# Softmax sums of a self-attention group inverted in a 128x8 tile that DMAs fill and empty

## The reference, cut to what matters

```
scores = jnp.einsum('bhqd,bhkd->bhqk', q, k) / math.sqrt(HD)
attn = jax.nn.softmax(scores, axis=-1)
out = jnp.einsum('bhqk,bhkd->bhqd', attn, v)
```

## Time and profile before

| | us |
|---|---|
| median of 3 runs | 260.71 |
| lowest, highest | 259.54, 261.23 |
| the profiled execution | 261.54 |
| its span, first to last instruction | 259.4 |

### The profile page before, as it was taken

One profiled execution on the slowest core, in us unless ns is written; L12 is line 12 of the kernel. 1 busy time (PEld: TensorE's weight loads), 2 busy tenths in 40 slices (PEclk: granted clock), 3 DMA queues, 4 the chain that ended last, 5 costly groups with the idle time before them and its releaser, 6 DMA issues.

```text
span 259.4 us, 4344 instructions
## 1 busy us (share of the span) xinstructions
PE 239.6 (92%) x1563; PEld 171.6 (66%) x1563; DVE 196.5 (76%) x351; ACT 132.2 (51%) x285; POOL 103.3 (40%) x135
## 2 busy tenths in 40 slices
PE   7999999988997799998999999999999999989971
PEld 4478797754654457675666767677776777668850
DVE  1377577899765899869889998986669895897574
ACT  1545377566368366556467656654435533313430
POOL 7297400000114307745466555556255533001362
PEclk9999999999999899999999999999999999999995
DMA  6999940000000840000000000000000000000011
GB/s 246 321 278 322 412 167 0 4 1 3 0 3 0 158 86 0 3 0 0 5 0 0 3 0 0 0 3 0 0 3 0 1 3 1 0 3 0 1 40 40
DMA packets 4500, 13.65 MB, mean 53 GB/s; under 512 B 512, under 2 KB 1280, under 8 KB 4352
## 3 DMA queue, kind: packets, MB, share of 16 engines
q1 hardware_dynamic: 4048, 11.29, 13.1%
q0 software_dynamic: 432, 2.10, 3.7%
HBM read 14.43 MB, written 0.52 MB: 58 GB/s over the span
## 4 chain that ended last, share of the span: by engine, by line
PE 71%; DVE 13%; DMA 5%; ACT 4%; issue 2%; SPq 2%; POOL 1%; POOLq 0%; DVEq 0%; ACTq 0%
PE ps L844 11%; PE ps L794 7%; PE ps L821 5%; PE ps L858 5%; PE ps L822 5%; PE ps L795 5%; PE ps L778 5%; DMA wq<-in_wq 5%; PE ps L634 3%; PE ps L923 3%; DVE mneg L1350 3%; PE ps L831 2%; PE ps L696 2%; PE ps L681 2%; PE ps L574 2%
## 5 line engine op out<-in xcount | busy, mean ns | idle before, releaser
L1184 ACT ACTIVATE probs<-ps 128x512 f32<-128x512 f32 x64 | 38.0, 597 | 46.7 <-PE ps L822 45.8
L1412 DVE TENSOR_REDUCE xmneg<-ps 128x1 f32<-128x512 f32 x64 | 43.0, 688 | 16.2 <-PE ps L795 15.8
L445 POOL TENSOR_TENSOR psums<-psums,probs 128x512 f32<-128x512 f32 x30 | 38.6, 1288 | 10.8 <-ACT probs L1184 8.3
L441 POOL TENSOR_TENSOR psums<-probs 128x512 f32<-128x512 f32 x15 | 19.2, 1281 | 43.1 <-ACT probs L1184 43.1
L794 PE MATMUL ps<-KA,QA 128*128 128x512 f32 x64 | 30.3, 474 | 2.8 <-DVE xmneg L1412 1.9
L844 PE MATMUL ps<-probs,kv_dup 128*64 128x256 f32 x256 | 31.2, 385 | 0.0
L1430 DVE RECIPROCAL xrcp<-ps 128x256 f32<-128x256 f32 x16 | 28.0, 1751 | 1.9 <-PE ps L831 1.9
L1176 ACT ACTIVATE QA<-ps 64x256 fp32r<-64x256 f32 x64 | 24.2, 378 | 10.1 <-PE ps L778 8.9
L1350 DVE TENSOR_REDUCE mneg<-ps 128x4 f32<-128x1024 f32 x16 | 19.6, 1224 | 9.4 <-PE ps L574 9.0
L821 PE MATMUL ps<-QA,KA 128*128 128x512 f32 x64 | 26.0, 406 | 0.0
L398 POOL TENSOR_TENSOR rstd<-mv,eps_col 128x1 f32<-128x1 f32 x12 | 2.3, 189 | 59.4 <-DVE mv L1338 59.1
(11 more groups left out here) (162 smaller groups left out, 459.7 us busy)
## 6 DMA issues: line engine op xcount, KB each, us to landing
wu<-in_wu SPq DMA_DIRECT2D x4, 640.0 KB, 8.9
wq<-in_wq SPq DMA_DIRECT2D x4, 512.0 KB, 13.4
wcT<-in_wcT SPq DMA_DIRECT2D x4, 384.0 KB, 12.3
wE<-in_wE SPq DMA_DIRECT2D x4, 320.0 KB, 11.2
w13T<-in_w POOLq DMA_DIRECT2D x1, 1024.0 KB, 8.2
x1T<-in_xT SPq DMA_DIRECT2D x1, 512.0 KB, 3.7
kvp<-in_kv POOLq DMA_DIRECT2D x1, 512.0 KB, 6.1
x_nat<-in_xn SPq DMA_DIRECT2D x1, 512.0 KB, 18.6
```

What stands on the lines that cost most here:

```text
L445: g.tensor_tensor(psums[:, s, :], psums[:, s, :], probs[:, s, kc, :], ALU.add).then_inc(xadd_sb, 1)
L1184: a.activation(probs[:, n % 2, kc, :], ps[:, 2 + u % 2, :], ACT.Exp).then_inc(xexp_sb, 1)
L1412: v.tensor_reduce(xmneg[:, n % 4, qt, hh:hh + 1], ps[:, u % 2, :], AX.X, ALU.max, negate=True).then_inc(xmax_sb, 1)
```

## The change

For seven of the eight groups (`TURNED`) the order is turned round: the sums are inverted first and spread afterwards. SP sends the four sum rows of `CT` (one partition, 256 elements each) by four DMAs into `sum_cols`, a tile of 128 partitions by 8. DVE inverts that (`attn_recip`), SP sends the result back by four DMAs into four rows of `rcp_rows`, a 128x256 tile that is zero elsewhere, and PE spreads those rows with `sel` (`attn_rcp`, at j = 3, or at r = 3 of units 0 to 2, ahead of `query`). DVE multiplies `CT` by the result straight from PSUM (`attn_norm`). Both small tiles and `rcp_rows` have two buffers. Group 3 (`DIRECT`) keeps the old way. The small reciprocal stands at j = 1, or behind the second maximum of a unit; the multiply at j = 3, or behind the fourth maximum.

```diff
+TURNED = [0, 1, 2, 4, 5, 6, 7]
+DIRECT = 3
...
+        sum_cols = sb("sum_cols", [P, 2, NE])
+        rcp_cols = sb("rcp_cols", [P, 2, NE])
...
-        rcp = sb("rcp", [P, SEQ], scope=early)
+        rcp_rows = sb("rcp_rows", [P, 2, SEQ], scope=early)
...
+            def sums_to_cols(k):
+                i = TURNED[k]
+                b, g = i // NQUAD, i % NQUAD
+                sp.wait_ge(ct_sb, i + 1)
+                if k >= 2:
+                    sp.wait_ge(rcp_sb, k - 1)
+                for hh in range(4):
+                    row = slice(32 * hh + HD, 32 * hh + HD + 1)
+                    sp.dma_start(sum_cols[32 * hh:32 * hh + 32, k % 2, :], CT[row, g, b * SEQ:(b + 1) * SEQ]).then_inc(cols_in[k % 2], 16)
+
+            def cols_to_rows(k):
+                sp.wait_ge(rcp_sb, k + 1)
+                if k == 0:
+                    sp.wait_ge(rows_zero, 1)
+                if k >= 2:
+                    sp.wait_ge(sum_ps, TURNED[k - 2] + 1)
+                for hh in range(4):
+                    row = slice(32 * hh + HD, 32 * hh + HD + 1)
+                    sp.dma_start(rcp_rows[row, k % 2, :], rcp_cols[32 * hh:32 * hh + 32, k % 2, :]).then_inc(rows_in[k % 2], 16)
+
+            for k in range(len(TURNED)):
+                sums_to_cols(k)
+                cols_to_rows(k)
...
+            pool.wait_ge(stack_ps, 6)
+            g.memset(rcp_rows[:], 0.0).then_inc(rows_zero, 1)
...
                 if i >= 1:
-                    pe.wait_ge(sums_sb, i)
+                    pe.wait_ge(ct_sb, i)
+                if i == DIRECT + 1:
+                    pe.wait_ge(sums_sb, 1)
+                elif i >= 2:
+                    pe.wait_ge(cn_sb, i - 1)
...
+            def attn_rcp(i):
+
+                k = TURNED.index(i)
+                if k == 0:
+                    pe.wait_ge(consts, 7)
+                pe.wait_ge(rows_in[k % 2], 64 * (k // 2 + 1))
+                if i >= 1:
+                    pe.wait_ge(cn_sb, i)
+                if i < NGRP - 1:
+                    pe.wait_ge(ct_sb, i + 2)
+                pe.matmul(ps[:, 4, SEQ:2 * SEQ], sel[:], rcp_rows[:, k % 2, :], start=True, stop=True).then_inc(sum_ps, 1)
...
-                    if i >= ALAG + 2 and j == 0:
-                        attn_sum(i - ALAG - 2)
+                    if i == DIRECT + ALAG + 2 and j == 0:
+                        attn_sum(DIRECT)
...
+                    if i >= ALAG + 2 and j == 3 and i - ALAG - 2 != DIRECT:
+                        attn_rcp(i - ALAG - 2)
...
-                    if n < 3 and r == 0:
-                        attn_sum(NGRP - 3 + n)
                     if n < NUNIT:
                         xmax(n, r)
+                    if n < 3 and r == 3:
+                        attn_rcp(NGRP - 3 + n)
...
+            def attn_recip(i):
+
+                k = TURNED.index(i)
+                dve.wait_ge(cols_in[k % 2], 64 * (k // 2 + 1))
+                if k >= 2:
+                    dve.wait_ge(rows_in[k % 2], 64 * (k // 2))
+                v.reciprocal(rcp_cols[:, k % 2, :], sum_cols[:, k % 2, :]).then_inc(rcp_sb, 1)
+
             def attn_norm(i):
 
                 b, g = i // NQUAD, i % NQUAD
-                dve.wait_ge(sums_sb, i + 1)
-                if i >= 1:
-                    dve.wait_ge(cn_sb, i)
-                v.reciprocal(rcp[:], sums[:]).then_inc(rcp_sb, 1)
-                dve.wait_ge(rcp_sb, i + 1)
                 c = slice(b * SEQ, (b + 1) * SEQ)
-                v.tensor_tensor(CN[:, g, c], CT[:, g, c], rcp[:], ALU.mult).then_inc(cn_sb, 1)
+                dve.wait_ge(sum_ps, i + 1)
+                v.tensor_tensor(CN[:, g, c], CT[:, g, c], ps[:, 4, SEQ:2 * SEQ], ALU.mult).then_inc(cn_sb, 1)
...
                 if n < NUNIT:
                     xmax(n, 1)
+                if n < 3:
+                    attn_recip(NGRP - 3 + n)
                 if n < NUNIT:
                     xmax(n, 2)
-                if n < 3:
-                    attn_norm(NGRP - 3 + n)
                 if n < NUNIT:
                     xmax(n, 3)
                     xmax_split(n)
+                if n < 3:
+                    attn_norm(NGRP - 3 + n)
```

More of the change, by code:

```diff
@@ L131, in decoder_layer @@
         sums = sb("sums", [P, SEQ], scope=early)
-        rcp = sb("rcp", [P, SEQ], scope=early)
-        sb("behind_dense", [P, 13 * T - 2 * NQUAD * T - 2 * SEQ], scope=early)
+        rcp_rows = sb("rcp_rows", [P, 2, SEQ], scope=early)
+        sb("behind_dense", [P, 13 * T - 2 * NQUAD * T - 3 * SEQ], scope=early)
         V1 = sb("V1", [P, NT, NH, 32], scope=early)
@@ L235, in decoder_layer @@
         sum_ps = sem("sum_ps")
+        rows_zero = sem("rows_zero")
         sums_sb = sem("sums_sb")
+        cols_in = [sem(f"cols_in{k}") for k in range(2)]
         rcp_sb = sem("rcp_sb")
+        direct_sb = sem("direct_sb")
+        rows_in = [sem(f"rows_in{k}") for k in range(2)]
         cn_sb = sem("cn_sb")
@@ L621, in attn_sum @@
             def attn_sum(i):
+                pe.wait_ge(cn_sb, i)
                 b, g = i // NQUAD, i % NQUAD
-                if i == 0:
-                    pe.wait_ge(consts, 7)
                 pe.wait_ge(ct_sb, i + 1)
                 pe.matmul(ps[:, 4, SEQ:2 * SEQ], sel[:], CT[:, g, b * SEQ:(b + 1) * SEQ], start=True, stop=True).then_inc(sum_ps, 1)
+            def attn_rcp(i):
[4 more added lines that the diff above has]
+                if i >= 1:
+                    pe.wait_ge(cn_sb, i)
+                if i < NGRP - 1:
+                    pe.wait_ge(ct_sb, i + 2)
+                pe.matmul(ps[:, 4, SEQ:2 * SEQ], sel[:], rcp_rows[:, k % 2, :], start=True, stop=True).then_inc(sum_ps, 1)
             def attn_proj(t, o, gs):
@@ L839, in xpv @@
                 if kc == 0 and n < 2:
-                    pe.wait_ge(sums_sb, NGRP)
+                    pe.wait_ge(cn_sb, NGRP)
                 if kc == 0 and n >= 2:
@@ L1090, in attn_sums_out @@
                 act.wait_ge(sum_ps, i + 1)
-                if i >= 1:
-                    act.wait_ge(rcp_sb, i)
                 a.activation(sums[:], ps[:, 4, SEQ:2 * SEQ], ACT.Copy).then_inc(sums_sb, 1)
@@ L1146, in _ @@
                         attn_exp(i - ALAG, j // 2)
-                    if i >= ALAG + 2 and j == 0:
-                        attn_sums_out(i - ALAG - 2)
+                    if i == DIRECT + ALAG + 2 and j == 0:
+                        attn_sums_out(DIRECT)
                     if i >= ALAG + 1 and j == 2:
@@ L1224, in _ @@
                         attn_exp(NGRP - 1, r // 2)
-                    if n < 3 and r == 0:
-                        attn_sums_out(NGRP - 3 + n)
                     if n < 2 and r == 2:
@@ L1313, in context_lo, with attn_norm_direct @@
                 v.tensor_tensor(KA[DC:P, ks], ps[DC:P, 4, :], KA[DC:P, ks].bitcast(F32), ALU.subtract).then_inc(kvT_lo, 1)
+            def attn_recip(i):
[4 more added lines that the diff above has]
+                v.reciprocal(rcp_cols[:, k % 2, :], sum_cols[:, k % 2, :]).then_inc(rcp_sb, 1)
             def attn_norm(i):
                 b, g = i // NQUAD, i % NQUAD
-                dve.wait_ge(sums_sb, i + 1)
-                if i >= 1:
-                    dve.wait_ge(cn_sb, i)
-                v.reciprocal(rcp[:], sums[:]).then_inc(rcp_sb, 1)
-                dve.wait_ge(rcp_sb, i + 1)
-                c = slice(b * SEQ, (b + 1) * SEQ)
-                v.tensor_tensor(CN[:, g, c], CT[:, g, c], rcp[:], ALU.mult).then_inc(cn_sb, 1)
+                c = slice(b * SEQ, (b + 1) * SEQ)
+                dve.wait_ge(sum_ps, i + 1)
+                v.tensor_tensor(CN[:, g, c], CT[:, g, c], ps[:, 4, SEQ:2 * SEQ], ALU.mult).then_inc(cn_sb, 1)
+            def attn_norm_direct(i):
+                b, g = i // NQUAD, i % NQUAD
+                c = slice(b * SEQ, (b + 1) * SEQ)
+                dve.wait_ge(sums_sb, 1)
+                v.reciprocal(sums[:], sums[:]).then_inc(direct_sb, 1)
+                dve.wait_ge(direct_sb, 1)
+                v.tensor_tensor(CN[:, g, c], CT[:, g, c], sums[:], ALU.mult).then_inc(cn_sb, 1)
             def norm_stats(k, t, src, base):
@@ L1389, in _ @@
                         max_split(i)
-                    if i >= ALAG + 2 and j == 0:
-                        attn_norm(i - ALAG - 2)
+                    if i >= ALAG + 2 and j == 1 and i - ALAG - 2 != DIRECT:
+                        attn_recip(i - ALAG - 2)
+                    if i == DIRECT + ALAG + 2 and j == 0:
+                        attn_norm_direct(DIRECT)
                     if i in (2, 3) and j == 1:
@@ L1399, in _ @@
                         norm_apply(0, j - 2, x1)
+                    if i >= ALAG + 2 and j == 3 and i - ALAG - 2 != DIRECT:
+                        attn_norm(i - ALAG - 2)
             def query_lo(n):
```

## The result

The changed kernel takes 285.55 us (median of 4 executions, 284.22 to 287.31) against 260.91 for the kernel before: 1.097 times as long, 95% interval 1.0925 to 1.101. The forecast was slower, but by 8.4 us (269.1 us, range 264.0 to 274.0); it was 24.6. The kernel before was run once more beside it, which moved its median from 260.71 to 260.91. A few executions, of several kernels, took clearly longer than the others of the same kernel, and the ratios leave them out.

The account below looks back on a forecast made before the run. PE was taken to set the time overall, with DVE's reciprocal on the chain in steps 4 to 6. Terms 1.4 - 0.1 + 5.5 + 0.7 + 0.9 = +8.4 us gave 269.1 us on the median, range 264.0 to 274.0.

Parts of the forecast that it names:

- DVE's relief: Seven groups lose the large reciprocal on DVE: 11 us less busy, able to count only in steps 4 to 6.
- the trip's 3 x 0.45 for the issues: SP issues a trip's four DMAs in a row, 0.45 us apart; part of the 3.32 us trip.
- the contention of unit 0: Rows delayed by bulk loads in cross-attention unit 0: no term given; unit 0 was forecast at +0.6 us.
- one fall of the clock at +0.9: Units 1 and 2: PE's idle time brings one more fall to 1.2 GHz, some 3.5 us long; +0.9 us.
- two additions: Rows queueing beside the w2T load in unit 1, +0.7 us, and one more fall of PE's clock, +0.9 us.
- upper end of the trip, 4.02: Longest trip from small reciprocal to last row landed, with a 2.4 us landing: 4.02 us against 3.32 expected.
- its 2.0 us: Fixed part of a DMA by the Trainium skill; the prediction said the 1.7 us store contradicts it mildly.
- SP's queue as a ring: Steps: SP's issues and a landing from one reciprocal to the next, put at 5.1 us, below every new step length.
- Contention: Cross-attention unit 1: the four rows may queue behind pieces of the w2T load, 0 to 2 us, taken as 0.7.
- Rival A: Steps and units: not slower, as the trip is short; for a 2.0 us trip +0.9 us, 261.6 us; chance 8%.
- Rival B: Seven trips: slower still, with 2.4 us landings, full contention and full clock loss; 276.2 us; chance 12%.

Follow-up runs that it names:

- late_fill: Changed kernel with w13T and w2T loads issued in unit 6 and 8 or 14 dummy matmuls ahead of PE's wait for the rows; ratio 1.0855.
- late_loads: Changed kernel with the w13T and w2T loads issued in unit 6 instead of before unit 0; 279.96 us, ratio 1.0761.
- cols_by_act: Change for groups 0, 1, 2 and 4 only, with the first trip's four DMAs issued from ACT's queue instead of SP's; ratio 1.0338.
- one_late: Changed kernel with one DMA each way per group instead of four, and the w13T and w2T loads issued in unit 6; 263.27 us, ratio 1.0103.
- steps_only: Changed kernel with the change for groups 0, 1, 2 and 4 only, all others the old way; 268.41 us, ratio 1.0291.
- best_steps: Changed kernel with one DMA each way, for groups 0, 1, 2 and 4 only, all others the old way; ratio 0.997.
- one_dma: Changed kernel with one DMA each way per group in place of four; 266.38 us, ratio 1.0217.

## Why the prediction was wrong

**What held.** The sign, and most of the mechanism: in steps 4 and 6 and in the units PE, in order, stands at attn_rcp until the rows land (in step 5 it does not wait). A landing was taken at 1.7 us and is 1.7. The small reciprocal was 0.20 us for 0.17. DVE's relief was 9.6 us for 11, and nothing came of it in this kernel. Behind query(4) the kernel only shifts (+0.6).

**Where the miss lies.** Three terms of the sum failed: the trip's 3 x 0.45 for the issues, the contention of unit 0 put at nothing, and one fall of the clock at +0.9. Without its two additions the forecast had +6.8 us up to query(4); +22.8 was measured, 16 more. By the trace of the changed kernel 10.6 of these are the trips: from the small reciprocal to the 0/1 matmul they take 3.9, 4.1, 4.3 and 4.3 us in the steps and 9.5, 3.8 and 3.8 in the units, where each was to take 3.32. Of the 10.6, 5.7 are the one late landing (7.42 for 1.7) and 4.9 the rest, mostly the issues. The other 5.4 us are instructions of PE and what waits for them: the reciprocal comes later in a step or unit, and the matmuls around it take longer, nearly all at the lower clock; 0.7 is the wait for the first trip in step 4. This split says where the time lies, not what each cause alone would give back; for that see the runs.

**The issue pitch**, the term 3 x 0.45, was mis-sized: 0.62 us, so the trip is 3.86 us and not 3.32, and single issues of up to 1.1 us make two trips of 4.3. I had taken the pitch from large loads, which have another form. My upper end of the trip, 4.02, held the 3.86 only because of the 2.4 us landing in it. Three waits of 0.62 are as long as a landing, as expected against the rule on issues that the prediction cites. On its 2.0 us the prediction drew the wrong conclusion: the Trainium skill ("DMA: Bandwidth & Descriptors", Anatomy of one DMA) fits that figure to DMAs issued by GpSimd. The trips' DMAs are issued by SP, so a landing of 1.7 us does not speak against it.

**SP's queue as a ring** was argued away wrongly too: "SP needs, from one reciprocal to the next, 0.27 + 7 x 0.45 + 1.7 = 5.1 us, below every new step length". With eight issues at 0.62 and a last landing of up to 3.1 us it is 7.75 us (late_fill), above the 6.17 forecast for a step. In the changed kernel this limit cost only the 0.7 us in step 4; in steps 5 and 6 PE's slow clock hid it, and it showed when late_fill took the slow clock away. I compared it with the step lengths once and did not ask what it does if two of its sizes are wrong.

**Contention** was looked for in the wrong unit. I gave unit 1 0 to 2 us for it, from 91% busy DMA engines, and unit 0 nothing, without setting the trip's times beside the issue of the loads. The trace of before had it:

```profile
84.12 0.65 POOL L425 DMA_DIRECT2D w13T<-in_w  x1 [2.48 <-ACT probs L1086]
```

That is inside the trip that I put at 83.25 to 86.57. Two of the four rows were issued after w13T and took 7.0 to 7.4 us; late_loads shows the price, 5.6 us. In unit 1, where I had looked, the loads had landed and the last row took 1.7. It was also the size of the effect that was off: I had thought of a small piece waiting behind one piece of a load.

The Trainium skill ("DMA: Bandwidth & Descriptors", Queues, rings and completion order) says that a DMA engine takes turns between its queue rows packet by packet. By that I would expect DMAs of 1 KB to be held for a packet or a few. The trace here does not bear that out: 6.9 to 7.4 us beside w13T and w2T, 1.7 alone.

**The clock.** I expected one more fall and +0.9 us. It was low in step 5 (0.50), step 6 (0.73) and units 0 and 1 (0.66, 0.74), and PE's busy time grew 11.7 us. But what restoring it gives back was near my small term, not near that sum: at full clock throughout the steps, late_fill takes 45.20 to 68.46, 23.3 us, and the changed kernel 24.1, so 0.8 us in the steps. Most of the slow work lies where PE would have waited for the rows or, behind them, for SP's queue. Two limits lay close together, and each of two edits met only one: late_fill restored the clock and met SP's queue, cols_by_act relieved SP's queue, which at the slow clock was not the limit. Step 5 shows the trap: by its window PE is busy 100%, yet at the full clock it takes 7.23 us instead of 8.08, where the kernel before took 5.68. Only 0.85 of the 2.4 us lost are the clock.

**Rival A** gave the point from which the change would win in steps 5 and 6: a trip under 2.83 us. one_late has 2.0 (unit 2) and wins there, 5.02 and 5.20 us against 5.68, near the 4.85 that rival A gave to a trip of 2.0. The nearness is part luck: at 55.61 the 0/1 matmul starts straight behind PE's products, so step 5 is now held by PE's own work and no longer by the trip. Its prices for the units, 0.43, 0.8 and 1.5 us, were somewhat low (0.5, 1.4, 2.2). Rival B, at 276.2, came nearest in time, with a wrong split: it put 4.9 us into slow landings in all seven places, where there was one, in unit 0.

What stays open: why a small DMA beside a bulk load lands 5 to 8 us late, and how the 24.6 us divide between issues and clock in the units, where no run separates them cleanly.

## What to carry to other kernels

A step that leaves for another engine by DMA costs its issues too, one after the other: count them for each trip, and count all issues of the queue from one turn of the loop to the next, at the pitch of this form of DMA. Four DMAs where one would do were the difference between a loss of 7.6 us (steps_only) and no loss (best_steps, 0.997) in the same four groups. Set the times of a small transfer beside those of every bulk load. Ask where in its stream the waiting engine stands when the trip begins; a trip of even 2.0 us has no place 1.0 us ahead of its use.

## What the runs showed of the hardware

- A DMA between SBUF tiles, 1 KB in 32-byte pieces, lands 1.7 us after its issue. One of 4 KB over 128 partitions, in the same pieces, is no slower: in unit 2 of one_late it is issued at 99.14 and released PE at 100.92.
- Its issue on SP takes mostly 0.54 to 0.59 us (median 0.59, single ones up to 1.7), where a 128 KB store takes 0.34 and a 640 KB load 0.43: an issue is not cheaper because little is moved. One of 4 KB takes 0.54.
- Small DMAs issued by SP 0.3 to 4 us after a 1 MB load, beside it and a load of 0.5 MB, took 6.9 to 7.4 us to land in place of 1.7; the 4 KB one of one_dma, issued at 83.82 beside the same loads, released DVE 9.4 us later.
- Four dummy matmuls in a wait of 0.8 us kept the clock at its higher level through a stretch where it fell to the lower for some 3.5 us in the kernel before. Over whole executions the mean granted clock was 0.989 to 0.999 with them and mostly 0.980 to 0.995 in the kernel before.
